# Two-layer graph attention: layer 1 packs the neighbours of two tiles into seven shared chunks

## The reference

```python
q = x @ Wq.T + bq
k = x @ Wk.T + bk
v = x @ Wv.T + bv
scores = q @ k.T / jnp.sqrt(d)
scores = jnp.where(adj > 0, scores, neg)
att = jax.nn.softmax(scores, axis=-1) @ v
return jax.nn.elu(att)
```

## Time and profile before

| what | us |
|---|---|
| median of 3 runs | 1687.95 (1686.07 to 1689.5) |
| the profiled execution, own time | 1688.92 |
| its span | 1687.2 |
| POOL busy | 1132.0 |
| PE busy | 1204.0 |
| DVE busy | 1189.1 |
| ACT busy | 938.6 |
| mean granted TensorE clock | 0.696 of full speed |

### The profile page before, as it was taken

One profiled execution on the slowest core, in us unless ns is written; L12 is line 12 of the kernel. 1 busy time (PEld: TensorE's weight loads), 2 busy tenths in 40 slices (PEclk: granted clock), 3 DMA queues, 4 the chain that ended last, 5 costly groups with the idle time before them and its releaser, 6 DMA issues.

```text
span 1687.2 us, 23399 instructions
## 1 busy us (share of the span) xinstructions
PE 1204.0 (71%) x5503; PEld 952.4 (56%) x5554; DVE 1189.1 (70%) x6433; ACT 938.6 (56%) x1955; POOL 1132.0 (67%) x1206
## 2 busy tenths in 40 slices
PE   2657887777877777877766476776777777776765
PEld 1344555555555555655546365666666666666664
DVE  3557899888888888888887355655665565566555
ACT  2769888888888888888853233223323332332322
POOL 1237777667666666666675577777777777777773
PEclk9778777777777777777765566666566556556655
DMA  9869999999999999999922122222222222222221
GB/s 287 342 223 393 397 399 398 400 400 400 399 397 388 384 382 381 388 384 393 359 62 55 52 59 66 62 61 65 65 64 65 64 66 63 64 66 64 66 66 40
DMA packets 113048, 368.10 MB, mean 218 GB/s; under 512 B 33553, under 2 KB 58642, under 8 KB 80146
## 3 DMA queue, kind: packets, MB, share of 16 engines
q1 hardware_dynamic: 66242, 285.50, 43.6%
q0 software_dynamic: 38464, 81.08, 17.2%
q10 hardware_dynamic: 8208, 0.03, 0.3%
HBM read 353.80 MB, written 12.72 MB: 217 GB/s over the span
## 4 chain that ended last, share of the span: by engine, by line
POOL 34%; DMA 31%; issue 13%; DVE 9%; PE 7%; ACT 5%; SPq 1%; POOLq 0%; ACTq 0%; DVEq 0%
POOL arena L596 33%; DMA arena<-in_adj_dram 29%; ACT arena L1158 4%; PE psum L1370 2%; DMA table<-arena 1%; PE psum L1431 1%; DVE arena L860 1%; POOL arena L567 1%; PE psum L1403 1%; SPq L452 1%; PE psum L1417 1%; DVE arena L653 1%; DVE arena L693 0%; DVE arena L755 0%; DVE arena L752 0%
## 5 line engine op out<-in xcount | busy, mean ns | idle before, releaser
L567 POOL DMA_INDIRECT arena<-table,arena x576 | 552.4, 959 | 246.5 <-issue 162.2
L596 POOL DMA_INDIRECT arena<-table,arena x576 | 551.2, 957 | 184.0 <-issue 184.0
L1158 ACT ACTIVATE arena<-arena 128x2048 bf16<-128x2048 int32 x256 | 486.9, 1902 | 98.1 <-DMA arena<-in_adj_dram 97.4
L1370 PE MATMUL psum<-arena 128*128 128x512 bf16 x973 | 283.1, 430 | 56.8 <-ACT arena L1158 51.1
L860 DVE SCALAR_TENSOR_TENSOR arena<-arena 128x131 f32<-128x131 f32 (+1 forms) x768 | 266.3, 347 | 15.2
L1417 PE MATMUL psum<-arena 128*128 128x131 f32 (+1 forms) x768 | 200.6, 433 | 103.9 <-ACT arena L1305 102.2
L1403 PE MATMUL psum<-arena 128*128 128x18 f32 x768 | 142.8, 318 | 148.2 <-DVE arena L823 147.8
L1417 PEld LDWEIGHTS psum<-arena 128*128 128x128 f32 x768 | 179.5, 329 | 107.6 <-issue 107.6
L1403 PEld LDWEIGHTS psum<-arena 128*128 128x128 f32 x768 | 136.2, 261 | 166.7 <-DVE arena L823 166.4
L1370 PEld LDWEIGHTS psum<-arena 128*128 128x128 bf16 x1024 | 111.3, 117 | 192.3 <-issue 70.5
L1410 PE MATMUL psum<-arena 128*128 128x1 f32 x768 | 140.7, 299 | 96.1 <-DVE arena L843 96.1
(11 more groups left out here) (203 smaller groups left out, 2067.9 us busy)
## 6 DMA issues: line engine op xcount, KB each, us to landing
arena<-in_adj_dram SPq DMA_DIRECT2D x256, 1024.0 KB, 22.4
arena<-table,arena POOLq DMA_INDIRECT x1152
table<-arena POOLq DMA_DIRECT2D x32, 132.0 KB, 3.5
table<-arena SPq DMA_DIRECT2D x16, 256.0 KB
arena<-table SPq DMA_DIRECT2D x64, 64.0 KB, 1.9
out_dram<-arena SPq DMA_DIRECT2D x16, 256.0 KB, 2.4
arena<-in_x_dram SPq DMA_DIRECT2D x4, 0.5 KB, 12.4
arena<-in_L_gnn_W_dram SPq DMA_DIRECT2D x1, 64.0 KB
```

What stands on the lines that cost most here:

```text
L567: pool.indirect_dma_start(Gt[:, v % GROUP, c + 1, :], None, table0, bass.IndirectOffsetOnAxis(idx_all[:, v, c:c + 1], 0))\
L596: pool.indirect_dma_start(Gt[:, t % GROUP, c + 1, 0:D], None, table1, bass.IndirectOffsetOnAxis(idx_all[:, t, c:c + 1], 0))\
L1158: nc.scalar.activation(mask[:, k, q * QUARTER:(q + 1) * QUARTER], adj_sb[:, k, q, :], ACT.Relu, accum_out=sum_all[:, bass.ds(tile, 1), q:q ...
L1370: nc.tensor.matmul(V[k], shifted[:, s, :], mask[:, k, s * 512:(s + 1) * 512], start=(s == 0), stop=False)
```

## The change

Layer 1 gets a division of its own. Rows have REGULAR1 = 5 regular slots, and up to 19 surplus neighbours (OVER1). Each tile has four chunks of packed columns (512), but the last chunk of an even tile and the first of the odd tile after it are one gather: the even tile fills its columns from the left, the odd one from the right (its distances are mirrored), so a pair has 4 + 4 - 1 = 7 packed gathers and 2 x 5 regular ones, 17 in place of 18. The shared chunk lies in the even tile's buffer (`chunk_row`). Layer 0 keeps its six slots and three chunks.

The packed indices for layer 1 are not those of layer 0, so they are dealt again inside layer 1, two steps ahead: DVE splits the pair's lists into two BF16 halves (`halve`), makes `mine` in BF16 (`mark1`), PE deals owners and lists in BF16 (`deal1`: per chunk one product of 128 columns and two of 20), ACT copies owners and `mine` to f32, DVE picks one slot for each packed column (`pick1`), and the indices of the pair go to POOL, which waits for them after the five regular gathers of the even tile. The query product (`spread_u`) has one set of PSUM banks in place of two and stands behind the scatter on PE. `hot1`, `owned1`, `mine1` are rings of eight tiles. `scatter1`, `spread_max1`, `sum_up1`, `weigh_owners` are as before with four chunks; `add_slots1` has one slot fewer. In layer 0 one DVE copy per pair keeps the lists (`lists_all`); near the flag two operations count, four split and five judge again. The programs of layer 1 start one group earlier (g = -1), in which the first tiles are dealt. `y` has one buffer in place of two.

```diff
+REGULAR1 = 5
+OVER1 = SLOTS - REGULAR1
+OWN1 = 1 + REGULAR1
+CHUNKS1 = 4
+QCOLS1 = CHUNKS1 * 128
+SHARED = 7 * 128
...
-        own_ps = [bank(k)[:, 0:CHUNKS * P].rearrange("p (c q) -> p c q", c=CHUNKS) for k in range(2)]
-        uq_ps = [bank(2 + k)[:, 0:CHUNKS * DE].rearrange("p (c d) -> p c d", c=CHUNKS) for k in range(2)]
+        own_ps = bank(0).rearrange("p (c q) -> p c q", c=CHUNKS1)
+        lists_ps = bank(1)[:, 0:CHUNKS1 * LISTED1].rearrange("p (c j) -> p c j", c=CHUNKS1)
+        uq_ps = [bank(2 + c // 2)[:, DE * (c % 2):DE * (c % 2 + 1)] for c in range(CHUNKS1)]
+        by_slot1_ps = [bank(6)[:, 32 * k:32 * k + OVER1] for k in range(2)]
+        max1_ps = [bank(6)[:, 64 + 8 * k:64 + 8 * k + CHUNKS1] for k in range(2)]
...
+        def chunk_row(t, c):
+            r = t % GROUP
+            return Gt[:, r - 1, ROWS - 1, 0:DE] if r % 2 and c == 0 else Gt[:, r, OWN1 + c, 0:DE]
...
+                def fetch(r, row, idx):
+                    pool.indirect_dma_start(Gt[:, r, row, 0:D], None, table1, bass.IndirectOffsetOnAxis(idx, 0))\
+                        .then_inc(rows_in[r], 16)
+                for pair in range(PAIRS):
+                    t, r = 2 * pair, 2 * pair % GROUP
                     pool.wait_ge(summed, T + t - 3)
-                    for c in range(ROWS - 1):
-                        pool.indirect_dma_start(Gt[:, t % GROUP, c + 1, 0:D], None, table1,
-                                                bass.IndirectOffsetOnAxis(idx_all[:, t, c:c + 1], 0))\
-                            .then_inc(rows_in[t % GROUP], 16)
+                    for c in range(REGULAR1):
+                        fetch(r, 1 + c, idx_all[:, t, c:c + 1])
+                    pool.wait_ge(idx_done, T + pair + 1)
+                    for c in range(CHUNKS1 - 1):
+                        fetch(r, OWN1 + c, idx_pair[:, pair, c:c + 1])
+                    pool.wait_ge(summed, T + t - 2)
+                    fetch(r, OWN1 + CHUNKS1 - 1, idx_pair[:, pair, CHUNKS1 - 1:CHUNKS1])
+                    for c in range(REGULAR1):
+                        fetch(r + 1, 1 + c, idx_all[:, t + 1, c:c + 1])
+                    for c in range(1, CHUNKS1):
+                        fetch(r + 1, OWN1 + c, idx_pair[:, pair, CHUNKS1 + c:CHUNKS1 + c + 1])
...
+                nc.vector.tensor_scalar(lists_all[:, at, 0:OVER1], dealt[:, r:r + 2, LISTED + REGULAR1:LISTED + SLOTS], 0.0, None, ALU.max)\
+                  .then_inc(count_kept, 1)
...
+                def halve(pair):
+                    def after(n):
+                        dve.wait_ge(halves_done, 3 * pair + n)
+                    lists = lists_all[:, 2 * pair:2 * pair + 2, :]
+                    to = halves[:, pair % 2, :, :, :]
+                    nc.vector.tensor_scalar(moved1[:, :, :], lists, BY128, None, ALU.add).then_inc(halves_done, 1)
+                    after(1)
+                    nc.vector.tensor_scalar(to[:, :, 0, :], moved1[:, :, :], -BY128, None, ALU.add).then_inc(halves_done, 1)
+                    after(2)
+                    nc.vector.tensor_tensor(to[:, :, 1, :], lists, to[:, :, 0, :], ALU.subtract).then_inc(halves_done, 1)
+                def mark1(v):
+                    dve.wait_ge(dist_done, T + v + 1)
+                    at_least(dve, mine1_done, v - 3)
+                    nc.vector.tensor_scalar(mine16[:, v % 4, :], dist1[:, v % 2, :], len5[:, v:v + 1], None, ALU.is_lt)\
                       .then_inc(mine_done, 1)
+                PICK1_STEPS = 4
+                def pick1(v):
+                    k, pair = v % 2, v // 2
+                    def after(n):
+                        dve.wait_ge(pick_done, PICK_STEPS * T + PICK1_STEPS * v + pair + n)
+                    dve.wait_ge(deal_done, T + v + 1)
+                    nc.vector.tensor_tensor(slot1[:, k, :], iota_q[:, k, :], lists_ps[:, :, OVER1], ALU.subtract).then_inc(pick_done, 1)
+                    after(1)
+                    nc.vector.tensor_tensor(hot1[:, v % RING, :, :], one(iota_over).to_broadcast([P, CHUNKS1, OVER1]),
+                                            cut_k(slot1[:, k, :], OVER1), ALU.is_equal).then_inc(pick_done, 1)
+                    after(2)
+                    nc.vector.tensor_tensor(picked1[:, :, :], hot1[:, v % RING, :, :], lists_ps[:, :, 0:OVER1], ALU.mult)\
+                      .then_inc(pick_done, 1)
+                    after(3)
+                    nc.vector.tensor_reduce(chosen[:, k, :], picked1[:, :, :], AX.X, ALU.add).then_inc(pick_done, 1)
+                    if k:
+                        after(4)
+                        nc.vector.tensor_tensor(chosen[:, 0, CHUNKS1 - 1:CHUNKS1], chosen[:, 0, CHUNKS1 - 1:CHUNKS1], chosen[:, 1, 0:1],
+                                                ALU.add).then_inc(pick_done, 1)
+                        after(5)
+                        nc.vector.tensor_scalar(idx_pair[:, pair, :], chosen.rearrange("p k c -> p (k c)"), 0.0, float(N), ALU.max, ALU.min)\
+                          .then_inc(idx_done, 1)
...
-                def score1(u, b, k, n):
-                    dve.wait_ge(rows_in[b], 16 * (ROWS - 1) * n)
-                    dve.wait_ge(self_in[b], 16 * (n - G))
+                def score1(u, b, k, g):
+                    if b % 2:
+                        dve.wait_ge(rows_in[b - 1], 16 * ((ROWS - 1) * G + (OWN1 - 1 + CHUNKS1) * (g + 1)))
+                        dve.wait_ge(rows_in[b], 16 * ((ROWS - 1) * G + (OWN1 - 1 + CHUNKS1 - 1) * (g + 1)))
+                    else:
+                        dve.wait_ge(rows_in[b], 16 * ((ROWS - 1) * G + (OWN1 - 1 + CHUNKS1) * (g + 1)))
+                    dve.wait_ge(self_in[b], 16 * (g + 1))
                     dve.wait_ge(own_done, u + 1)
-                    for c in range(CHUNKS):
-                        ins = nc.vector.tensor_tensor_reduce(out=prod[:, OWN + c, :], in0=Gt[:, b, OWN + c, 0:DE],
-                                                             in1=uq_ps[k][:, c, :], scale=1.0, scalar=0.0, op0=ALU.mult,
-                                                             op1=ALU.add, accum_out=l10[:, k, OWN + c:OWN + c + 1])
+                    for c in range(CHUNKS1):
+                        ins = nc.vector.tensor_tensor_reduce(out=prod[:, OWN1 + c, :], in0=chunk_row(u, c),
+                                                             in1=uq_ps[c], scale=1.0, scalar=0.0, op0=ALU.mult,
+                                                             op1=ALU.add, accum_out=l10[:, k, OWN1 + c:OWN1 + c + 1])
                     ins.then_inc(score_done, 1)
...
+                            if (t + 3) % 2 == 0:
+                                halve((t + 3) // 2)
+                            mark1(t + 3)
+                        if live(t, -2):
+                            pick1(t + 2)
...
-                            measure_spans(t + 1)
+                        if live(t, -3):
+                            v = t + 3
+                            if v >= 2:
+                                act.wait_ge(mine_done, T + v - 1)
+                            nc.scalar.activation(dist1[:, v % 2, :], iota_odd[:, :], ACT.Abs, bias=mid5[:, v:v + 1]).then_inc(dist_done, 1)
                         if live(t, 4):
                             act.wait_ge(rinv_done, T + t - 3)
                             nc.scalar.activation(accn[:, k, :], acc_sb[:, k, 0:D], ACT.Identity, scale=rinv[:, k, :])\
                               .then_inc(accn_done, 1)
-                        if live(t, 1):
-                            act.wait_ge(own_done, t)
-                            nc.scalar.activation(owned[:, (b - 1) % GROUP, :, :], own_ps[(b - 1) % 2], ACT.Identity)\
-                              .then_inc(owned_done, 1)
+                        if live(t, -2):
+                            v = t + 2
+                            act.wait_ge(mine_done, T + v + 1)
+                            nc.scalar.activation(mine1[:, v % RING, :], mine16[:, v % 4, :], ACT.Identity).then_inc(mine1_done, 1)
...
+                            act.wait_ge(deal_done, T + v + 1)
+                            nc.scalar.activation(owned1[:, v % RING, :, :], own_ps, ACT.Identity).then_inc(owned_done, 1)
...
+                def deal1(v):
+                    k, pair = v % 2, v // 2
+                    pe.wait_ge(mine_done, T + v + 1)
+                    pe.wait_ge(halves_done, 3 * pair + 3)
+                    at_least(pe, owned_done, T + v)
+                    if v >= 1:
+                        pe.wait_ge(pick_done, 5 * T + 4 * v + v // 2)
+                    for c in range(CHUNKS1):
+                        mine_c = mine16[:, v % 4, c * P:(c + 1) * P]
+                        nc.tensor.matmul(own_ps[:, c, :], mine_c, ident16[:, :], start=True, stop=True)
+                        nc.tensor.matmul(lists_ps[:, c, :], mine_c, halves[:, pair % 2, k, 0, :], start=True, stop=False)
+                        last = nc.tensor.matmul(lists_ps[:, c, :], mine_c, halves[:, pair % 2, k, 1, :], start=False, stop=True)
```

(32 more changed lines are left out.)

226 lines of the change are left out of this document (161 added, 65 removed).

## The result

The changed kernel takes 1662.5 us (median of 4 runs, 1653.1 to 1683.3), the kernel before 1687.9 us beside it (1686.1 to 1689.5). The run of 1683.3 us lies 1.8% over the quickest, counts as a slow one and is left out of the ratio, which is 0.983, 95% interval [0.981, 0.986]. The forecast was 1761 us and slower; what came is the rival C, less than its full 40 us.

What follows compares the result with a forecast made beforehand. GpSimd's gathers bound layer 1 at 11.36 us a tile; after the change TensorE's ring would, at 12.87. 63 steps add 95.0 us, then -4, -20 and +2 on 1688.9 give 1762 (median 1761), range 1672 to 1800.

Steps and rivals of the forecast that it cites:

- rival C: Layer 1: clock rises as often as before, ring 10.4 us under POOL's 10.73, 1650 up to 1688 us; chance 0.23.
- POOL's gain: Layer 1 gathers on GpSimd: 32 fewer at 1.262 us each, 40.4 us, the whole possible gain.
- The ring: TensorE's strict order of work per layer 1 step, 10.83 us at 1.2 GHz before, nearly a second bound behind POOL's 11.36.
- VectorE's longer work: DVE in layer 1: 8.3 us a step, 9 in odd steps, below 10.7 and so hidden.
- Layer 0 and the first tiles' dealing: List copies (6 us of DVE) hidden under layer 0's full DMA; dealing the first two tiles hidden, 0 to 3 us if not.
- the ring's sum: TensorE's layer 1 step at 1.2 GHz after the change: 12.87 us, 2.1 above the new POOL time.
- dealing, 12 BF16: Dealing on TensorE in layer 1: twelve BF16 instructions at 0.107 us, 1.28 us, bounds 0.56 and 2.57.
- output and query products, 6: Output and query products on TensorE, before the spread of the maximum: 2.22 us; the ring's only slack counted as 0.44.
- handover: From TensorE's spread of the maximum through DVE and ACT to the next weighted sum: 1.90 us, +0.30 for the fourth chunk included.
- I expect it in about one step of ten: TensorE's rise to 2.4 GHz in layer 1: six rises, -20 us, because the change cuts the wide f32 run.
- 3.3 us for 3.3 us: One clock rise in layer 1 gives 3.3 us at double pace, so it saves at most 3.3 us.
- ring theory: Experiments' theory: TensorE's 12.0 us ring at 1.2 GHz, over the gathers' 10.7, costs time; allowed after_16 at most 10 us less.

Runs made afterwards that it cites:

- fill_gap_c: Changed kernel plus four unread FP32 products in TensorE's handover, where the kernel before takes 1685.8 us: 1642.3 us, ratio 0.974 to the kernel before.
- fill_before: Kernel before plus the same four unread products behind the spread of the maximum: 2050.7 us beside 2044.8, ratio 1.003.
- deal_u_gap_c: Changed kernel with dealing and query product moved behind the spread of the maximum, into TensorE's handover: 2020.6 us, 8.5 under the changed kernel beside it.
- fill_gap_d: Changed kernel plus four unread products in the handover, on a chip where the kernel before takes 2025.1 us: 1991.9 us, ratio 0.984.
- after_16: Changed kernel with one more gather of each pair left out (16 a pair): 1977.7, 1981.1 and 1984.8 us in three groups, 0.968 of the kernel before each.
- before_17: Kernel before without the ninth gather of odd tiles (17 a pair), nothing added: 2003.5, 2006.6 and 2012.8 us in three groups.
- after_c: Changed kernel as it is, third group, where the kernel before takes 2051.4 us: 2029.1 us.

## Why the prediction was wrong, point by point

**What held.** POOL's gain: 40.4 us forecast, 41.4 measured. The ring as the next to be tight, VectorE waiting for the spread of the maximum in place of rows: 123.2 us in 53 tiles. VectorE's longer work is hidden: 7.87 us busy in a 12.0 us step (forecast 8.3), the new mark 0.35 us where 0.55 was taken. Layer 0 and the first tiles' dealing cost nothing in the profiled execution (first gather 3.4 us earlier).

**The first step that failed is the ring's sum: 12.87 us, 0.86 too long.** From start to start in the step above, at 1.2 GHz:

| term | forecast | measured |
|---|---|---|
| weighted sum, 8 | 1.86 | 1.85 |
| two turns | 0.43 | 0.43 |
| dealing, 12 BF16 | 1.28 | 0.68 |
| queries, 8 | 1.71 | 1.86 |
| scatter, 8 | 1.57 | 1.71 |
| output and query products, 6 | 2.22 | 1.88 |
| spread of the maximum, 8 | 1.90 | 1.71 |
| handover | 1.90 | 1.89 |
| sum | 12.87 | 12.01 |

The forecast column is the earlier trace rows with the forecast's additions. The largest error is the dealing. I took 0.107 us an instruction, by analogy with the one-column FP32 products; the rows give 0.10 behind a product of 128 columns in the first round and 0.08 or less behind one of 20, 0.68 / 12 = 0.057 on the mean. The bounds were 0.56 and 2.57, and the truth lies by the lower one. The Trainium skill ("TensorE: Matmul & The Clock Gate", Back-to-back issue gap) gives columns over 1.2 GHz, which makes the 0.56, but for a product by itself; where each has a weight load, it says, both set the spacing. The trace lies between, nearer to the 0.56 than to my choice. What I held against it was an FP32 row, whose products are two instructions each and follow 0.21 us apart at 1 and 19 columns and 0.23 at 129. The second is the 0.34 us of the output and query products: I had counted slack only from the end of the last one. But an instruction's recorded end lies behind the point at which the next can start (L1780 is 0.80 long and the next product starts 0.59 after it), so a wait of 0.44 in the profile hides more slack than 0.44.

This alone does not turn the sign. With 12.01 in the place of 12.87 the forecast's sum is 1762 - 63 x 0.86 = 1708 us, still 1% slower.

**The second step that failed is "I expect it in about one step of ten".** The forecast allowed the high clock six rises, 20 us. The granted clock over layer 1 stayed at 0.60 (0.61 before), which is 20% of 700 us, 140 us of it high. The argument was that the change cuts the unbroken run of wide FP32 products, which had come before the rise that I had looked at. One rise is no rule: in the kernel after six steps in a row, with the same instructions, stay at 0.50, and the seventh and eighth stand at 0.88. Those 140 us pay less than the forecast's "3.3 us for 3.3 us": 63 steps at 12.01 are 756.6 us, and from the first weighted sum (957.7) to the last (1640.1) they took 682.4, so 74 us for 140. The handover does not quicken (1.89 at either clock), and a quick step then runs into the gathers, as the 13 waits of L1233 show.

**The two weigh the same, and the sign needs both.** The ring's sum was 54 us too long, and the relief by the clock 74 - 20 = 54 too small. With only the clock put right the sum is 1708 as well; with both it is 1762 - 108 = 1654, and the profiled execution took 1653.1. That it closes so well proves little, since the 74 us are themselves what is left of the 63 steps. Rival C's number came in part by luck: it took the ring as 0.86 us too long and the relief as 2.5 us a step, where 74 / 63 = 1.2 was measured, and the two errors go against each other. Its mechanism, a clock that stays and GpSimd that never stops, is what the trace shows.

The Trainium skill (same page, The HAM clock gate) says that activity releases the throttle. fill_gap_c and fill_before agree (0.60 to 0.70, 0.60 to 0.66). The change itself does not: TensorE is busy 563 us of 700 where it was 508 of 712, and the clock is 0.60 after 0.61. Nor does deal_u_gap_c (0.58 to 0.50 with TensorE busy 476 us of 600 in place of 430, though a low clock also makes the same work busy for longer), nor fill_gap_d (0.60 with 508 us busy). What decides it is open. The chance of 0.23 for rival C was too small: I had no measurement by which a kernel whose TensorE works as much as before would lose the high clock, and rival C needed nothing but that it stay.

**What is shown and what is only argued.** Shown where the kernel before takes 1686 us, by the profiled executions: the gathers' gain, the ring of 12.0 us at 1.2 GHz, the clock that stayed, and the 9 us by which the end of the kernel after lags behind its gathers. That this lag comes from TensorE is backed by fill_gap_c, in which it is gone, with the reservation that the kernel after did not run beside it. Argued only: why the clock stayed, and how after_16, before_17 or a shorter ring would behave there; these ran on the other chips alone, where the ring theory's forecasts for them failed.

## What to carry to other kernels

Where one engine's ring lies 10% over the pace that feeds it, sum it at either clock and ask what share of the time at the high clock breaks even; then take the share that the profile of before shows, unless a measurement speaks for another. Price an unmeasured kind of instruction at both ends and carry both into the sum, above all when the row used as an analogy has another data type. Where the last steps lag behind what feeds them and TensorE idles in each handover, a few unread products in that idle time are worth one run; where the ring did not set the pace they brought nothing or cost 0.3%. And where steps alternate, compare pairs: a step as long as the bare ring is no proof that the ring costs time.

## What the runs showed that I had not expected

- Twelve BF16 products with a weight load each (128, 20, 20 columns) run in 0.68 us at 1.2 GHz, 57 ns each, where the instructions of FP32 products follow 0.21 us apart at 1 and 19 columns and 0.23 at 129.
- With unread work in TensorE's idle time the kernel was 1.0% faster by the ratios to the kernel before (0.974 against 0.983, not measured side by side), with the granted clock of the layer at 0.70 in place of 0.60.
- TensorE's clock fell from 0.58 to 0.50 over 600 us when the dealing and the query product moved from the ring into its idle time, in all three traces of that kernel.
- On the chips where the kernel before takes over 2000 us, a pair of steps takes 26.3 us with the change's work and without it: the 12.0 us steps cost nothing there.
- The same program takes 1686 to 1688 us in two sets of runs and 2025 to 2051 on four other chips. Each gather is as long (947 ns), but GpSimd waits some 2.8 us for a buffer in 59 of 64 tiles, and the reading of the adjacency runs slower, as a line of the page shows for after_c (GB/s in 40 slices; 380 to 400 on the first chip):

```profile
GB/s 313 291 289 317 305 328 320 301 312 323 320 304 308 320 328 299 319 310 327 300 65 47 45 34 47 53 55 53 53 53 54 53 54 53 54 53 48 53 55 29
```
